# An attention and feed-forward layer on eight cores: first-sequence tokens loaded ahead of the weights, query weights cast on GpSimd, value weights ahead of projection

## The chip, the cores and the metric

The kernel runs on all 8 cores of one Trainium2 chip. Each core takes two of the 16 sequences, by itself; the cores exchange nothing. The metric is the device time of the slowest core in microseconds (us). Each core has TensorE (matmuls), VectorE, ScalarE and GpSimd, and SyncE (SP), which here issues every transfer. The profile calls them PE (PEld for its weight loads), DVE, ACT, POOL and SP.

## The reference

One layer on x of 16 x 2048 x 1024, 32-bit floats. The softmax is over the 1024 x 1024 matrix of channels (one head, summed over the 2048 tokens), and norm follows norm:

```python
x = x + attn(layernorm(x))
x = x + ffn(layernorm(x))

def attn(x, ...):
    h = (x - mu) / sqrt(var + 1e-5) * norm_w + norm_b
    q, k, v = split(h @ qkv_w.T + qkv_b)            # each 2048 x 1024
    w = softmax(einsum('ncq,nck->nqk', q, k / sqrt(2048)), axis=2)
    a = einsum('nqk,nck->ncq', w, v)
    return a @ proj_w.T + proj_b + x

def ffn(x, ...):
    h = fix8(x @ w1 + b1)                           # 1024 -> 4096, multiples of 2^-8
    h = piecewise linear gelu of h (33 points on [-4, 4]), fix8
    return fix8(h @ w2 + b2)                        # 4096 -> 1024
```

## The kernel before, in words

All engines run programs written out by hand, each in its own order, tied by semaphores. The names below are those of the profile.

**Sequence 0, start.** A sequence is 16 tiles of 128 tokens x 1024 channels (512 KB). A tile comes from `xs` into one of six slots of `ring` (32-bit). VectorE takes its statistics (`stats`, L722 and L725), ScalarE the root (L993), VectorE the reciprocal and `nms` = -mean/std (`finish_stats`, L729 and L731), and ScalarE writes the normalised tile to `Z` in 16 bits (L1003), which frees the slot. All slots are used in one order, counted by a position u: position u waits until the user of position u - 6 is done (`wait_slot`). TensorE adds each Z tile to the Gram matrix Z^T Z (L395: 11 matmuls a tile for most of it; a twelfth piece of 16 matmuls follows at the end because it reuses a bank). VectorE evicts it scaled by norm_w into `gm` (L750). GpSimd adds the 16 Z tiles into `acc` (L1200), from which TensorE makes column sums (L411).

**Weights.** The query (`wq`), key (`wk`), projection (`pw`) and value (`wv`) weights come as 8 tiles of 512 KB each through the same six slots and are cast to 16 bits: wq and wk on ScalarE (L1134), pw and wv on GpSimd (L1205). SP issues, in this order: the 16 x tiles with the first 4 wq tiles and nwb (norm_w as 512 KB) between them, the other 4 wq tiles, 8 wk tiles, two rows of biases, 16 stores of Z to `zscr`, `nbb` and `rbb`, 8 pw tiles, 8 wv tiles.

**Stages of sequence 0 on TensorE.** T1 = gm x wq: 16 tiles (L424), the first 8 mixed with transposes of gm (L404) that ScalarE copies back (`mirror`, L1015); VectorE and ScalarE evict T1 in turns. Column sums stand between T1 tiles 11 and 12; VectorE makes the columns `colq`, `colk` of them (L768 to L774). Then matvecs with wq and wk (L432, L439); scores, 8 tiles of 16 + 2 matmuls (L452, L457) in two pairs of banks; for each, VectorE takes the maximum (L797), `mxb` (L800), then `junk` (L814), which multiplies a value-weight tile in its slot by nbb and sums (`bias_v`), and scales the exponentials of ScalarE (L1039) to `wsm` (L806). The M stage (wsm x pw, L470 and L480: the first group of 4 tiles goes through the 8 softmax tiles qt in turn, and needs pw tile qt), then the N stage (M x wv, L501, L513, L520). Then the out stage, 16 tiles (L531) that read the transposed Z, `zt`.

**Sequence 1 beside it.** During M and N of sequence 0, VectorE and ScalarE take statistics and normalise the 16 x tiles of sequence 1, one between each two evictions, and GpSimd sums them. SP stores each Z tile, issues a transposed load (L264, from `zscr` to `zt`, of sequence 0) after every second one, and loads the next x tile. The Gram matrix of sequence 1 and its column sums come just before and between the out tiles of sequence 0 (`gram_slot`). From there to the end of the program (T1, softmax, M, N and out of sequence 1, and the feed-forward of all 32 token tiles) nothing is changed.

A load of a wv tile's slot waits for both its cast (`g_wv`) and its `junk` (`v_bv`).

## Time and profile before

| | before |
|---|---|
| median of 3 runs (lowest, highest) | 1439.39 us (1436.79, 1488.41) |
| profiled execution | 1433.04 us |
| its span, slowest core (3) | 1431.5 us |
| spans of the other cores | 1422.0 to 1429.9 us |
| busy: TensorE, VectorE, ScalarE, GpSimd | 94%, 75%, 57%, 42% |
| mean granted clock of TensorE, core 3 | 0.984 |

The span goes from the first to the last instruction of a core. Times in rows are us from its start. A busy engine is one that executes, and a matmul's end is modelled. "Idle before" names what an engine waited for last. The profile is one execution, of the slowest core.

### The profile page before, as it was taken

What the parts mean: (1) busy time and instruction counts of PE and PEld (TensorE: products, weight loads), DVE (VectorE), ACT (ScalarE), POOL (GpSimd) and SP (SyncE); (2) the same over time, 40 slices, a digit from 0 to 9 for tenths busy, and PEclk for the clock granted to TensorE, in tenths of its full rate; (3) what the DMA queues carried; (4) which work ended last, traced back from release to release, by engine and by line L of the source; (5) the groups of instructions that cost most, each with busy time, mean ns of one, the idle gap of its engine ahead of it and who ended that gap; (6) DMA issues with size and microseconds to landing.
All of it is one profiled execution on the core that took longest, in us unless ns stands there. A gap on an engine that the chain in (4) does not pass through costs nothing.

```text
span 1431.5 us, 22191 instructions; the slowest of 8 cores (1422.0 to 1431.5 us)
## 1 busy us (share of the span) xinstructions
PE 1339.8 (94%) x6232; PEld 603.2 (42%) x6232; DVE 1073.8 (75%) x1664; ACT 813.2 (57%) x1303; POOL 602.7 (42%) x435
## 2 busy tenths in 40 slices
PE   5896998999999977799999999999999999999998
PEld 2342444444444423344444444444444444444443
DVE  5426884553326789998888889889889889888883
ACT  5531552451216756666766766666676765766660
POOL 0814253441646566534443433433443443443430
PEclk9998999999999999999999999999999999999999
DMA  8677696669998851321031021022023013002102
GB/s 271 187 230 238 159 265 205 220 231 203 335 297 288 293 171 45 74 79 33 16 82 52 15 75 60 16 60 74 16 38 95 2 38 95 16 26 64 30 16 96
DMA packets 124540, 171.93 MB, mean 120 GB/s; under 512 B 74620, under 2 KB 74620, under 8 KB 124420
## 3 DMA queue, kind: packets, MB, share of 16 engines
q1 hardware_dynamic: 124420, 170.52, 39.8%
q8 instruction: 52, 0.85, 0.2%
q14 instruction: 68, 0.56, 0.1%
HBM read 103.38 MB, written 50.33 MB: 107 GB/s over the span
## 4 chain that ended last, share of the span: by engine, by line
PE 58%; DVE 19%; issue 13%; DMA 4%; ACT 4%; SPq 1%; DVEq 1%; POOL 0%; ACTq 0%; POOLq 0%
PE pf L643 16%; PE pf L671 9%; PE pf L656 8%; PE pf L531 8%; DVE gb L947 6%; DVE rbits L939 4%; PE pf L452 3%; PE pf L424 3%; DVE rbits L950 3%; PE pf L480 3%; PE pf L395 2%; DVE ub L964 2%; DMA ring<-xs 2%; PE pf L520 1%; DVE bn L722 1%
## 5 line engine op out<-in xcount | busy, mean ns | idle before, releaser
L1246 POOL TENSOR_TENSOR gb<-gb,ga 128x512 f32<-128x512 f32 x256 | 363.7, 1421 | 515.1 <-ACT gb L1102 515.1
L656 PE MATMUL pf<-w,yt 128*128 128x512 bf16 x1024 | 261.2, 384 | 26.5 <-ACT yt L1110 25.0
L1110 ACT ACTIVATE yt<-rbits 128x512 bf16<-128x512 int32 x256 | 160.8, 628 | 213.4 <-DVE rbits L950 213.3
L950 DVE SCALAR_TENSOR_TENSOR rbits<-ga,gb 128x512 int32<-128x512 f32 x256 | 260.2, 1017 | 27.5 <-DVE gb L947 0.9
L643 PE MATMUL pf<-z2cmA,w 128*128 128x512 bf16 x1024 | 244.0, 383 | 16.7 <-ACT kb L1094 16.7
L671 PE MATMUL pf<-w,yt 128*128 128x512 bf16 x1024 | 251.9, 380 | 0.0
L643 PE MATMUL pf<-z2cmB,w 128*128 128x512 bf16 x1024 | 241.9, 379 | 0.0
L1094 ACT ACTIVATE kb<-pf,b1x 128x512 int32<-128x512 f32 x256 | 173.5, 678 | 89.7 <-PE pf L643 88.3
L947 DVE SCALAR_TENSOR_TENSOR gb<-rbits,gb 128x512 f32<-128x512 int32 x256 | 202.4, 791 | 3.3 <-POOL gb L1246 3.2
L939 DVE TENSOR_SCALAR rbits<-kb 128x512 int32<-128x512 int32 x256 | 148.8, 581 | 44.9 <-ACT kb L1094 44.6
L1102 ACT ACTIVATE gb<-kb,c 128x512 f32<-128x512 int32 x256 | 181.0, 707 | 0.0
L656 PEld LDWEIGHTS pf<-w,yt 128*128 128x128 bf16 x1024 | 99.9, 98 | 153.3 <-issue 38.2
L643 PEld LDWEIGHTS pf<-z2cmA,w 128*128 128x128 bf16 x1024 | 100.3, 99 | 143.0 <-issue 27.2
L942 DVE TENSOR_SCALAR kb<-kb 128x512 int32<-128x512 int32 x256 | 136.7, 534 | 27.9 <-DVE rbits L939 1.4
L1101 ACT ACTIVATE ga<-kb 128x512 f32<-128x512 int32 x256 | 157.4, 615 | 0.0
L671 PEld LDWEIGHTS pf<-w,yt 128*128 128x128 bf16 x1024 | 100.5, 98 | 121.8 <-issue 1.7
L643 PEld LDWEIGHTS pf<-z2cmB,w 128*128 128x128 bf16 x1024 | 100.2, 98 | 120.8
L531 PE MATMUL pf<-nn,zt 128*128 128x512 bf16 x512 | 115.1, 385 | 4.7 <-DMA zt<-zscr 3.6
L1205 POOL CAST w<-ring 128x1024 bf16<-128x1024 f32 x64 | 72.3, 1129 | 71.4 <-DMA ring<-w_h 71.3
L395 PE MATMUL pf<-Z 128*128 128x512 bf16 (+3 forms) x384 | 69.5, 340 | 24.9 <-ACT Z L1003 24.9
L1210 POOL TENSOR_TENSOR xo<-xo,rbb 128x1024 f32<-128x1024 f32 x32 | 75.3, 2358 | 15.8 <-ACT xo L1069 15.8
L531 PEld LDWEIGHTS pf<-nn,zt 128*128 128x128 bf16 x512 | 50.5, 99 | 66.7 <-issue 9.4
(93 smaller groups left out, 1108.0 us busy)
## 6 DMA issues: line engine op xcount, KB each, us to landing
ring<-xs SPq DMA_DIRECT2D x64, 512.0 KB, 5.7
ring<-w_h SPq DMA_DIRECT2D x64, 512.0 KB, 8.0
x1scr<-xo SPq DMA_DIRECT2D x32, 512.0 KB, 3.3
xh<-x1scr SPq DMA_DIRECT2D x64, 256.0 KB, 3.3
ys<-xh SPq DMA_DIRECT2D x64, 256.0 KB, 2.2
zscr<-Z SPq DMA_DIRECT2D x32, 256.0 KB, 5.4
z2scr<-z2b SPq DMA_DIRECT2D x32, 256.0 KB, 2.6
ring<-wq_h SPq DMA_DIRECT2D x8, 512.0 KB, 5.1
```

The source lines that it names most:

```text
L531: mm = t.matmul(bank(pair + h), zt[:, d, 128 * m:128 * (m + 1)], nn[:, d, 512 * h:512 * (h + 1)], start=(d == 0), stop=(d == 7))
L643: mm = t.matmul(bank(h_bank(n)), w1[:, 4 * (ft // 4) + j // 2, w1_col(ft, j)], z2cm[c % 2][:, j, :], start=(j == 0), stop=(j == 7))
L656: mm = t.matmul(bank(tt), y_tile(c, ft, tt), w2[:, ft, 0:512], start=(ft == 0), stop=(ft == 31))
L671: mm = t.matmul(bank(HALF1_BANKS[tt % 2]), y_tile(c, 8 * q + r, tt), w2[:, 8 * q + r, 512:1024], start=(r == 0 and q == 0), stop=(r == 7 a ...
L939: v.tensor_scalar(out=rbits[n % 4][:], in0=kb[n % 3][:], scalar1=63, scalar2=None, op0=ALU.bitwise_and).then_inc(S["v_bits"], 1)
L947: v.scalar_tensor_tensor(out=gb[n % 2][:], in0=rbits[n % 4][:], scalar=4.0, in1=gb[n % 2][:], op0=ALU.mult, op1=ALU.mult).then_inc(S["v_mu ...
L950: v.scalar_tensor_tensor(out=rbits[n % 4][:], in0=ga[n % 2][:], scalar=256.0, in1=gb[n % 2][:], op0=ALU.mult, op1=ALU.add).then_inc(S["v_h ...
L1094: a.activation(out=kb[n % 3][:], in_=bank(h_bank(n)), func=AF.Identity, bias=b1x[:, n % 32:n % 32 + 1], scale=256.0).then_inc(S["a_k"], 1)
L1101: a.activation(out=ga[n % 2][:], in_=kb[n % 3][:], func=AF.Gelu, scale=float(2.0 ** -8))
L1102: a.activation(out=gb[n % 2][:], in_=kb[n % 3][:], func=AF.Gelu, bias=c025[:], scale=float(2.0 ** -8)).then_inc(S["a_g"], 1)
L1110: a.activation(out=yt[:, r, q, :, :] if c % 2 == 0 else yt[:, r, :, q, :], in_=rbits[n % 4][:].rearrange("p (a b) -> p a b", a=4), func=AF ...
L1246: g_.tensor_tensor(out=gb[n % 2][:], in0=gb[n % 2][:], in1=ga[n % 2][:], op=ALU.subtract).then_inc(S["g_d"], 1)
```

## The change

The program of SP: all 16 x tiles come first, positions 0 to 15; then the small constants and nwb; then wq, wk, and now wv ahead of pw. nbb and rbb are loaded right behind wk. A wv tile's load is issued after every second store of Z. Two transposed loads stand between pw and the six first x tiles of sequence 1, two behind them, and the other four after the second, fourth, sixth and eighth store of Z of sequence 1. GpSimd casts wq, between additions 7 and 8 of its sum; the sum no longer waits for 13 tiles. ScalarE casts one wk tile after each of its first four T1 evictions and one after each of the other four. VectorE makes the columns after all its T1 evictions, forms nms with tensor_scalar (per-partition scalar sr, constant -1) where it used scalar_tensor_tensor, and finishes tile 0 before it takes the statistics of tile 1.

```diff
@@ sync_program
-                if p in X_AT:
-                    s.wait_ge(S["a_z"], X_AT[p] + 1)
-                elif p in Q_AT:
-                    s.wait_ge(S["a_wq"], Q_AT[p] + 1)
+                if p < U_WQ:
+                    s.wait_ge(S["a_z"], p + 1)
+                elif p < U_WK:
+                    s.wait_ge(S["g_wq"], p - U_WQ + 1)
...
-            for t in range(6):
-                load(x_pos(t), x_tile(t))
+            for t in range(16):
+                load(t, x_tile(t))
             for dst, src in ((ident[:], ident_h), (cols[:], cols_h), (c2[:], c2_h)):
                 s.dma_start(out=dst, in_=src).then_inc(S["d_const"], 16)
-            for t in range(6, 16):
-                load(x_pos(t), x_tile(t))
-                if t in (7, 9, 11, 13):
-                    load(q_pos((t - 7) // 2), wq_h[(t - 7) // 2])
...
-            for j in range(4, 8):
-                load(q_pos(j), wq_h[j])
+            s.dma_start(out=nwb[:], in_=nwb_h).then_inc(S["d_nwb"], 16)
+            for j in range(8):
+                load(U_WQ + j, wq_h[j])
             for j in range(8):
                 load(U_WK + j, wk_h[j])
...
             for t in range(16):
                 s.wait_ge(S["a_z"], t + 1)
                 store_z(t)
...
+                if t % 2:
+                    load(U_WV + t // 2, wv_h[t // 2])
+            for j in range(8):
                 load(U_P + j, p_h[j])
...
-            for j in range(8):
-                load(U_WV + j, wv_h[j])
+            s.wait_ge(S["d_zst"], 256)
+            load_zt(0, range(2))
             for t in range(6):
                 load(U_X1 + t, x_tile(16 + t))
-            s.wait_ge(S["d_zst"], 256)
+            load_zt(0, range(2, 4))
             for t in range(16):
                 s.wait_ge(S["a_z"], 16 + t + 1)
                 store_z(16 + t)
-                if t % 2 == 0:
-                    load_zt(0, [t // 2])
+                if t % 2 and t < 8:
+                    load_zt(0, [4 + t // 2])
@@ vector_program
-                v.scalar_tensor_tensor(out=nms[:, g:g + 1], in0=mv[:, g, 0:1], scalar=-1.0, in1=sr[:, g:g + 1],
-                                       op0=ALU.mult, op1=ALU.mult).then_inc(S["v_nms"], 1)
+                v.tensor_scalar(out=nms[:, g:g + 1], in0=mv[:, g, 0:1], scalar1=sr[:, g:g + 1], scalar2=-1.0,
+                                op0=ALU.mult, op1=ALU.mult).then_inc(S["v_nms"], 1)
...
-            for i in range(1, 12, 2):
+            for i in range(1, 16, 2):
                 t1_evict(0, i)
             columns(0, XB[0][3])
-            for i in (13, 15):
-                t1_evict(0, i)
@@ scalar_program
-                if g in (8, 10, 12, 14):
-                    cast(wq[:, (g - 8) // 2, :], q_pos((g - 8) // 2), "a_wq")
-            for j in range(4, 8):
-                cast(wq[:, j, :], q_pos(j), "a_wq")
...
                 if j % 2:
                     t1_evict(0, 7 - j)
+                    cast(wk[:, (7 - j) // 2, :], U_WK + (7 - j) // 2, "a_wk")
             for i in range(8, 16, 2):
                 t1_evict(0, i)
-                cast(wk[:, i - 8, :], U_WK + i - 8, "a_wk")
-                cast(wk[:, i - 7, :], U_WK + i - 7, "a_wk")
+                cast(wk[:, i // 2, :], U_WK + i // 2, "a_wk")
@@ gpsimd_program
-                if b == 0:
-                    g_.wait_ge(S["a_z"], 13)
...
-            accumulate(0)
+            accumulate(0, range(7))
+            for j in range(8):
+                cast(wq[:, j, :], U_WQ + j, "g_wq")
+            accumulate(0, range(7, 15))
+            for j in range(8):
+                cast(wv[:, j, :], U_WV + j, "g_wv")
             for j in range(8):
                 cast(pw[:, j, :], U_P + j, "g_p")
```

SP's queue where the last x tiles of sequence 0 are issued, before (`ring` is the slots, `xs` x, `wq_h` and `wk_h` the query and key weights; line numbers differ between the two kernels):

```order
L257 DMA ring_69<-wq_h 128x1024 [waits a_wq]
L257 DMA ring_70<-xs 128x1024 [waits a_z]
L257 DMA ring_71<-xs 128x1024 [waits a_z]
L257 DMA ring_72<-wq_h 128x1024 [waits a_wq]
L257 DMA ring_67<-xs 128x1024 [waits a_z]
L257 DMA ring_68<-xs 128x1024 [waits a_z]
L257 DMA ring_69<-wq_h 128x1024 [waits a_wq]
L257 DMA ring_70<-wq_h 128x1024 [waits a_z]
```

And of the change, from the last three x tiles on:

```order
L245 DMA ring_68<-xs 128x1024 [waits a_z]
L245 DMA ring_69<-xs 128x1024 [waits a_z]
L245 DMA ring_70<-xs 128x1024 [waits a_z]
L267 DMA ident<-ident_h 128x128
L267 DMA cols<-cols_h 128x56
L267 DMA c_106<-c_h 2x1
L268 DMA nwb<-nwb_h 128x1024
L245 DMA ring_71<-wq_h 128x1024 [waits a_z]
L245 DMA ring_72<-wq_h 128x1024 [waits a_z]
```

The x tiles moved ahead of all query weights, which now follow in a block of eight whose last two wait for GpSimd's casts (`g_wq`).

SP's queue from the last value-weight tiles to the x tiles of sequence 1, before (`g_wv` counts casts, `v_bv` the `junk` instructions):

```order
L257 DMA ring_70<-wv_h 128x1024 [waits g_p]
L257 DMA ring_71<-wv_h 128x1024 [waits g_wv,v_bv]
L257 DMA ring_72<-wv_h 128x1024 [waits g_wv,v_bv]
L257 DMA ring_67<-xs 128x1024 [waits g_wv,v_bv]
L257 DMA ring_68<-xs 128x1024 [waits g_wv,v_bv]
```

And of the change, from the fourth projection tile (`p_h`) on:

```order
L245 DMA ring_68<-p_h 128x1024 [waits g_wv,v_bv]
L245 DMA ring_69<-p_h 128x1024 [waits g_wv,v_bv]
L245 DMA ring_70<-p_h 128x1024 [waits g_wv,v_bv]
L245 DMA ring_71<-p_h 128x1024 [waits g_p]
L245 DMA ring_72<-p_h 128x1024 [waits g_p]
L252 DMA_TRANSPOSE zt<-zscr 128x2048 [waits d_zst]
L252 DMA_TRANSPOSE zt<-zscr 128x2048
L245 DMA ring_67<-xs 128x1024 [waits g_p]
L245 DMA ring_68<-xs 128x1024 [waits g_p]
```

The waits for `junk` moved from the x tiles of sequence 1 to the projection tiles, and two transposed loads stand before the first of those x tiles.

GpSimd at its start, before (`acc` is the sum, `d_ring` the landing of a slot):

```order
L1200 TENSOR_TENSOR acc<-Z 128x1024 [waits a_z]
L1200 TENSOR_TENSOR acc<-acc,Z 128x1024 [waits a_z,g_acc] x14
L1205 CAST pw<-ring_69 128x1024 [waits d_ring2]
L1205 CAST pw<-ring_70 128x1024 [waits d_ring3]
L1205 CAST pw<-ring_71 128x1024 [waits d_ring4]
```

And of the change:

```order
L1177 TENSOR_TENSOR acc<-Z 128x1024 [waits a_z]
L1177 TENSOR_TENSOR acc<-acc,Z 128x1024 [waits a_z,g_acc] x6
L1182 CAST wq<-ring_71 128x1024 [waits d_ring4]
L1182 CAST wq<-ring_72 128x1024 [waits d_ring5]
L1182 CAST wq<-ring_67 128x1024 [waits d_ring0]
L1182 CAST wq<-ring_68 128x1024 [waits d_ring1]
L1182 CAST wq<-ring_69 128x1024 [waits d_ring2]
L1182 CAST wq<-ring_70 128x1024 [waits d_ring3]
L1182 CAST wq<-ring_71 128x1024 [waits d_ring4]
L1182 CAST wq<-ring_72 128x1024 [waits d_ring5]
L1177 TENSOR_TENSOR acc<-acc,Z 128x1024 [waits a_z,g_acc] x8
L1182 CAST wv<-ring_69 128x1024 [waits d_ring2]
```

Eight casts moved into the sum, and the value casts come right behind it.

## Rows read from the trace of the kernel before

**Rows 1.** Timeline, TensorE: start, length (us), engine, line, operation, out<-in, count [idle before]

```profile
25.70 1.89 PE L395 MATMUL pf<-Z 128*128 128x512 bf16 x11 [0.49 <-ACT Z L1003]
...
46.64 11.49 PE L395 MATMUL pf<-Z 128*128 128x512 bf16 x49 [4.11 <-ACT Z L1003]
...
59.60 0.55 PE L404 MATMUL pf<-ident,gm 128*128 128x128 bf16 x7 [1.47 <-DVE gm L750]
...
81.88 1.84 PE L411 MATMUL pf<-ones,acc 128*128 128x1 f32 x16
...
90.58 3.61 PE L432 MATMUL pf<-wq,colq 128*2 128x512 bf16 x16
...
97.58 3.63 PE L452 MATMUL pf<-wk,t1m 128*128 128x512 bf16 x16
...
122.95 5.70 PE L452 MATMUL pf<-wk,t1m 128*128 128x512 bf16 x16 [12.75 <-ACT eb L1039]
...
145.49 7.08 PE L470 MATMUL pf<-pw,wsm 128*128 128x512 bf16 x32
...
204.20 3.19 PE L395 MATMUL pf<-Z 128*128 128x512 bf16 x14
...
214.96 1.90 PE L411 MATMUL pf<-ones,acc 128*128 128x1 f32 x16
...
220.47 6.42 PE L531 MATMUL pf<-nn,zt 128*128 128x512 bf16 x16 [3.62 <-DMA zt<-zscr]
```

**Rows 2.** Windows: stretch, length, busy time by engine (instructions), clock, DMA, GB/s

```profile
110.00:123.00 13.00, 0.25 (x2) 0.08 (x2) 5.92 (x7) 1.21 (x2) 9.09 (x9) 0.64 1.00 339
...
220.50:227.00 6.50, 6.50 (x19) 2.43 (x20) 0.00 (x0) 0.00 (x0) 0.99 (x1) 0.56 0.76 272
```

**Rows 3.** Timeline, VectorE, x tiles of sequence 0

```profile
17.54 1.29 DVE L722 BATCH_NORM_STATS2 bn<-ring 128x6 f32<-128x512 f32 x2
...
19.47 1.29 DVE L722 BATCH_NORM_STATS2 bn<-ring 128x6 f32<-128x512 f32 x2
```

**Rows 4.** Line 731 alone: VectorE's nms, duration min/median/max in ns, first and last start

```profile
L731 DVE SCALAR_TENSOR_TENSOR nms<-mv,sr x32: 158/160/1700, 9.6 to 209.4; 128x1 f32<-128x1 f32 x32
```

**Rows 5.** Timeline, ScalarE, normalised tiles of either sequence

```profile
21.54 1.24 ACT L1003 ACTIVATE Z<-ring,nms,sr 128x1024 bf16<-128x1024 f32 x1
...
208.74 2.37 ACT L1003 ACTIVATE Z<-ring,nms,sr 128x1024 bf16<-128x1024 f32 x2 [1.33 <-DVE nms L731]
```

**Rows 6.** Timeline, GpSimd: the sum of sequence 0, value-weight casts

```profile
42.97 31.61 POOL L1200 TENSOR_TENSOR acc<-acc,Z 128x1024 f32<-128x1024 f32 x14
...
123.03 3.56 POOL L1205 CAST wv<-ring 128x1024 bf16<-128x1024 f32 x3 [0.58 <-DMA ring<-wv_h]
```

**Rows 7.** Timeline, VectorE: column sums, T1, softmax and N stage

```profile
84.39 0.16 DVE L774 SCALAR_TENSOR_TENSOR colq<-cols,sc 128x8 bf16<-128x8 f32 x1
...
90.75 0.69 DVE L760 CAST t1m<-pf 128x512 bf16<-128x512 f32 x1 [2.76 <-PE pf L424]
...
116.87 2.07 DVE L814 SCALAR_TENSOR_TENSOR junk<-ring,nbb 128x1024 f32<-128x1024 f32 x1 [13.54 <-DMA ring<-wv_h]
...
125.94 0.15 DVE L800 TENSOR_SCALAR mxb<-mx 128x1 f32<-128x1 f32 x1
...
147.09 1.23 DVE L814 SCALAR_TENSOR_TENSOR junk<-ring,nbb 128x1024 f32<-128x1024 f32 x1
...
208.51 0.73 DVE L833 TENSOR_SCALAR nn<-pf,cols 128x512 bf16<-128x512 f32 x1
```

**Rows 8.** Timeline, SP's queue: transposed loads being issued

```profile
172.88 6.83 SPq L264 DMA_TRANSPOSE zt<-zscr  x1
...
316.11 33.08 SPq L264 DMA_TRANSPOSE zt<-zscr  x8
```

**Rows 9.** DMA issues, 0 to 260 us: count, KB each, us to landing

```profile
ring<-xs SPq DMA_DIRECT2D x44, 512.0 KB, 5.3
...
ring<-p_h SPq DMA_DIRECT2D x8, 512.0 KB, 11.2
```

51 lines of the change are left out of this document (20 added, 31 removed).

## The prediction, made before any run of the change

> **What bounds the kernel now.** I read the page first: TensorE is busy 94% of 1431.5 us, so only the places where it waits, or runs at half clock, can give time back. Then I read TensorE's timeline from its start [rows 1], because the change ends where the second sequence is under way. Up to there it loses time in four places. It follows the normalised tiles Z one by one (11 matmuls, 1.89 us, after each) and starts on the fourteenth only at 46.64; the Gram matrix ends at 58.1 and the next stage starts at 59.60. It stands 12.75 us before 122.95, in the score stage. It stands again up to 220.47, for the transposed Z. And after the two long stands the first 16 matmuls take 5.70 and 6.42 us, where 16 at full clock take 3.6: the granted clock was 0.64 of full during the first stand and 0.56 in the 6.5 us behind the second [rows 2], so a good part of those ran at the lower of its two levels (1.2 of 2.4 GHz).
>
> Next, who is waited for. The first loss is the supply of tiles: VectorE could start a tile's statistics every 1.93 us (17.54, 19.47), but four query-weight loads and nwb take places in the load queue between the tiles, and of the 32 nms instructions the longest takes 1.70 us where the median is 0.16: the long ones run while GpSimd sums [rows 3, 4, 6]. The second loss is one VectorE instruction: `junk`, which reads a value-weight tile in softmax tile 0, waits 13.54 us for its load [rows 7]; the value weights stand behind the 16 stores and 8 projection tiles on SP. The third loss is the last of eight transposed loads, plus a Z chain that lags: the N stage's matmuls end at 204.2, its last VectorE eviction starts only at 208.51 and the last Z ends at 211.1 [rows 1, 5, 7]. Behind 220 everything hangs on the out stage of sequence 0 through waits that move with it (w1 and w2 loads are issued after its stores), and nothing there is changed, so a shift at 220 should arrive whole at the end.
>
> **The change, step by step** (E is the end of the scores, N the end of the N stage's matmuls).
>
> 1. *Front.* All 16 tiles come at VectorE's 1.93 us: statistics of tile 15 start at 17.54 + 9 x 1.93 = 34.9. Z of a middle tile ends 5.2 us after its statistics start (17.54 to 21.54 + 1.24) [rows 3, 5]; the last has no following tile to wait through, which saves the 1.3 us of that tile's statistics: 38.8. A 512-column matmul takes 0.216 us in a run (32 in 7.08 less the last one's tail [rows 1]); the eleven of a tile have the columns of eight, 1.73 us, less than 1.93. So TensorE keeps up, then ends tile 15 at 40.5 and the sixteen 512-column matmuls of the last Gram piece at 44.0; with the 1.4 us of handover seen between 58.1 and 59.60 the T1 stage may begin at 45.4, that is 14.2 earlier. The query weights now come behind the tiles and nwb. Their last loads wait for GpSimd's first casts, eight tiles and nwb in a row at 1.55 us a tile (0.524 MB at the 339 GB/s of the fullest stretch [rows 2]): the last lands near 48.4, is cast (1.04 us and a handover) by 49.6, and T1's first tile ends at 49.9, where its seven transposes (0.55) and eight matmuls (1.73) alone would have ended it at 47.7. So 12.0 us are left of 14.2 [rows 1, 6]. Bounds: 14 if the casts keep up, 9 if the x tiles need about 0.3 us more each. The first seven additions of the sum (2.26 each by 31.61/14) and then the casts fit before this, and the other eight take 18.1, to 67.7; the column sums need them at 81.88 - 12.0 = 69.9 [rows 1, 6]. That cover is 2.2 us; beyond it, each late us costs one.
> 2. *Column sums read after all T1 evictions.* The query matvecs (90.58) wait for `columns`, which now stands behind the last eviction (90.75 + 0.69) and lasts 0.7 (83.9 to 84.55): they start at 92.2. Cost 1.6 us [rows 1, 7].
> 3. *Value weights ahead.* Key weights are cast between the mirrors, so value tiles 0 to 5 get slots well before softmax. The stand goes. Score tiles 3 to 7 take 145.49 - 122.95 = 22.54, less 5.70 - 3.63 for the clock, 4.09 each; eight in a row, with the 0.22 that tile 2 waits for the first exponential, take 32.9; they took 145.49 - 97.6 = 47.9. Gain 15.0, the half clock included.
> 4. *Projection weights behind them.* New wait: projection tile 5 takes the slot of value tile 7, so SP issues it after the last `junk`. This is E + 0.1 + 1.22 + 0.15 + 1.23 + handovers = E + 2.8 (145.49 to 148.3) [rows 1, 7]. At the median landing of x tiles, 5.3 us [rows 9], it lands at E + 8.1, tile 7 two places later at 11.2, is cast at 12.4, and the four matmuls of the last group end at E + 13.3. Now they end at E + 6.9. Cost 6.4. Bounds: 4 when the three land together and cast back to back, 12 at the 11.2 us landing that projection tiles have now [rows 9]; I stay near 5.3, since nothing else is in flight then.
> 5. *x tiles of sequence 1.* Behind those three loads SP now issues two transposed loads first (8 take 33.08 us, 4.1 each, the longest single one 6.83 [rows 8]). Tile 16 is then issued at E + 12.2 and lands at 17.5. VectorE and, behind it, ScalarE's next root and eviction wait; M tile 10 needs that eviction at E + 23.7 and has it by about 21.2. Cover 2.5 us, cost 0. Later tiles come two per transposed load, 1 to 3 us late on VectorE, which eight PSUM banks absorb.
> 6. *nms as tensor_scalar.* `mxb`, the same form (tensor_scalar, 128x1), takes 0.15 us at 125.94 while a GpSimd cast runs (three casts, 123.03 to 126.59) [rows 6, 7]; so nms should not wait either. VectorE then keeps up with TensorE: last eviction at N + 0.1 to 0.8, nms by 1.4, last Z at N + 2.9. From the last Z to the end of column sums it is 214.96 + 1.90 - 211.1 = 5.7 [rows 1, 5], so the out stage starts at N + 8.6, with all transposed loads long there; now it starts at 220.47 - 204.2 = 16.3. Gain 7.7. And without the long stand its first tile should run at full clock: 6.42 - 3.6 = 2.8.
> 7. Small collisions (value and projection casts against `junk` and `wsm`; key casts before mirrors on ScalarE): 1.2, an allowance; `junk` beside casts takes 2.07 where it takes 1.23 alone [rows 7], and a score tile leaves VectorE 0.4 us. The first nms made ahead of the second tile's statistics is worth nothing: TensorE gets one tile sooner and then waits for the second.
>
> On the port two sentences of the Trainium skill bear (SBUF — State Buffer, "Who interferes with whom"): a VectorE instruction with two SBUF inputs blocks against a GpSimd instruction that reads SBUF, and the trace agrees (nms up to 1.70 against 0.16 [rows 4]). But the page also lets tensor_scalar enter a 2-port mode that blocks the same way; by that rule nms would still wait, which is the second rival below.
>
> **Sum.** 12.0 + 15.0 + 7.7 + 2.8 = 37.5 gained; 1.6 + 6.4 + 1.2 = 9.2 lost; 28.3 us less. The profiled span goes from 1431.5 to about 1403. Its execution took 1433.0, below the three runs' median of 1439.4, so against the median: 1411.
>
> **Rivals.**
> - *The weights' wait grows* (0.14). Projection tiles land as late as now, or tile 16 beyond its cover: 6 to 10 us more than in steps 4 and 5. About 1420. For it: 5.3 is a median among x tiles, 11.2 the one of these very tiles. Against: those 11.2 were with 16 stores and two more loads in flight.
> - *nms still waits* (0.10). Then nms of a tile waits for the addition that the last Z released: about 2.2 [rows 6] plus Z's own 1.24 [rows 5], a pitch near 3.5 instead of 1.93 for the seven additions that now run during the x loads. That costs 7 x 1.6 = 11, and 3 more in step 6: 1425. Against: `mxb`. For: mxb has no scalar read from SBUF, nms has.
> - *Query weights late* (0.07): loads at 1.9 us each instead of 1.55 and a sum that misses its cover, 5 us: 1416.
> - *Better than the sum* (0.08): projection tiles land together, no collisions: 1405.
> - *Slower* (0.03). Eight transposed loads on SP stand ahead of x tile 13 of sequence 1, and each us more per transposed load delays it by eight. With 5 us each it comes about when needed (3 us of cover). At (28.3 + 3)/8 + 5 = 8.9 us each the whole gain is gone, and from 12.5 each the kernel is slower by 2%: 1468 or more. The longest now is 6.83 [rows 8].
>
> **Numbers.** The forecast has 0.58; its own range is 1405 to 1417. A measurement of this kernel tells about 2%, 28.8 us, from no change, and the forecast lies on that line: half of its chance (0.30) and the better case (0.08) make faster 0.38; the rest of it and the other rivals make the same 0.59; slower 0.03. The range reaches from the lower bounds of steps 1 and 4 to the second rival: 1402 to 1426.
>
> **What would show it.** Step 1: last Z near 39, T1's first tile ending near 49. Step 2: matvecs 1.6 after the last T1 tile. Step 3: no wait of `junk` for a load, scores without a gap. Step 4: a gap of 6 us in the first M group, released by a GpSimd cast. Step 5: VectorE's first statistics of sequence 1 waiting some 5 us for x, with TensorE unhurt. Step 6: all nms near 0.16, the out stage within 9 us of the N stage. Wrong would be: nms above 1 us, a gap in the M stage beyond the first group, or a front that ends later than 53.

## The result, and the profile after

| | before | after |
|---|---|---|
| median of 4 runs each, on one chip | 1439.97 us | 1423.88 us (1422.85 to 1496.78) |
| profiled execution | 1433.04 us | 1423.3 us |
| its span, slowest core | 1431.5 us (core 3) | 1421.8 us (core 4) |
| median span of its eight cores | 1427.1 us | 1416.0 us |

The ratio after to before is 0.9892, with an interval of 0.9874 to 0.991: 1.1% or 15.5 us less (the two medians are 16.1 us apart), faster but by less than 2%. The prediction said 1411 with a range of 1402 to 1426; the forecast's own range, 1405 to 1417, was missed. Span against span, the sum promised 28.3 us and 9.7 came. Since single cores differ by 9 to 10 us, the table below gives the start of each stage as a median over cores. Here and in all that follows, such medians, of stage starts and of spans, leave out cores that ran a whole execution at a granted clock below 0.98, which happened with every kernel, in 10 to 42 of 100 cases; the time of an execution, being that of its slowest core, contains them.

| start, us | T1 stage (first matmul with wq) | query matvecs | M stage | N stage's end | out stage | span |
|---|---|---|---|---|---|---|
| before | 57.4 | 88.0 | 144.1 | 203.0 | 218.2 | 1427.1 |
| after | 48.8 | 83.9 | 123.9 | 190.1 | 207.6 | 1416.0 |

From the out stage to the end both take 1209 us in the median of the cores (1207 to 1212 on single ones), so a shift there does arrive whole at the end, as predicted.

TensorE's timeline of the kernel after, core 4, from its T1 stage to the out stage of sequence 0. The columns are those of [rows 1]: start, duration, line, what it does, count, and in brackets the idle time before it and who ended it.

```profile
49.98 0.55 PE L387 MATMUL pf<-ident,gm 128*128 128x128 bf16 x7 [1.49 <-DVE gm L733]
52.64 0.38 PE L407 MATMUL pf<-wq,gm 128*128 128x512 bf16 x1 [0.81 <-POOL wq L1182]
53.98 0.38 PE L407 MATMUL pf<-wq,gm 128*128 128x512 bf16 x1 [0.97 <-POOL wq L1182]
...
61.12 0.33 PE L387 MATMUL pf<-ident,gm 128*128 128x128 bf16 x3 [0.32 <-ACT gm L998]
...
86.75 5.30 PE L415 MATMUL pf<-wq,colq 128*2 128x512 bf16 x16 [2.44 <-DVE colq L757]
...
95.44 3.63 PE L435 MATMUL pf<-wk,t1m 128*128 128x512 bf16 x16
...
128.46 3.63 PE L453 MATMUL pf<-pw,wsm 128*128 128x512 bf16 x16
133.37 1.02 PE L453 MATMUL pf<-pw,wsm 128*128 128x512 bf16 x4 [1.29 <-POOL pw L1182]
136.66 1.87 PE L453 MATMUL pf<-pw,wsm 128*128 128x512 bf16 x4 [2.27 <-POOL pw L1182]
...
141.73 20.94 PE L463 MATMUL pf<-pw,wsm 128*128 128x512 bf16 x94
...
169.49 1.02 PE L484 MATMUL pf<-mm__51,wv 128*128 128x512 bf16 x4 [0.77 <-ACT mm__51 L1028]
...
194.52 2.75 PE L378 MATMUL pf<-Z 128*128 128x512 bf16 x11
...
201.12 0.59 PE L378 MATMUL pf<-Z 128*128 128x512 bf16 x1 [2.16 <-ACT Z L986]
...
204.79 6.47 PE L378 MATMUL pf<-Z 128*128 128x512 bf16 x33 [0.55 <-ACT Z L986]
...
213.07 3.40 PE L514 MATMUL pf<-nn,zt 128*128 128x512 bf16 x15
```

Against [rows 1]: the stand of 12.75 us in the score stage is gone, and the scores run from 95.44 to 128.46. Two new stands are there for `pw` in the first M group. The N stage ends at 194.5, and then TensorE goes tile by tile behind Z, as it once did at the start; the out stage comes 18.6 us after N's end, where before it came 16.3 after. (Some matmuls can be missing from a trace: x15 where 16 ran.)

The other engines on the same core, in the order of the stages: SP's queue, whose rows say how long an issue held it, then VectorE and ScalarE.

```profile
132.75 8.33 SPq L252 DMA_TRANSPOSE zt<-zscr  x2
141.18 4.17 SPq L245 DMA_DIRECT2D ring<-xs  x6
145.40 13.11 SPq L252 DMA_TRANSPOSE zt<-zscr  x2
158.61 0.53 SPq L248 DMA_DIRECT2D zscr<-Z  x1
159.23 0.38 SPq L245 DMA_DIRECT2D ring<-xs  x1
...
160.13 5.66 SPq L252 DMA_TRANSPOSE zt<-zscr  x1
...
16.25 1.29 DVE L705 BATCH_NORM_STATS2 bn<-ring 128x6 f32<-128x512 f32 x2 [2.52 <-DMA ring<-xs]
...
85.65 0.89 DVE L756 CAST colk<-sc 128x8 bf16<-128x8 f32 x1
...
148.22 1.29 DVE L705 BATCH_NORM_STATS2 bn<-ring 128x6 f32<-128x512 f32 x2 [6.34 <-DMA ring<-xs]
...
165.39 1.29 DVE L705 BATCH_NORM_STATS2 bn<-ring 128x6 f32<-128x512 f32 x2 [2.59 <-DMA ring<-xs]
...
195.08 1.29 DVE L705 BATCH_NORM_STATS2 bn<-ring 128x6 f32<-128x512 f32 x2 [3.53 <-DMA ring<-xs]
...
40.03 2.37 ACT L986 ACTIVATE Z<-ring,nms,sr 128x1024 bf16<-128x1024 f32 x2
...
202.28 2.37 ACT L986 ACTIVATE Z<-ring,nms,sr 128x1024 bf16<-128x1024 f32 x2
```

SP stood in two transposed loads from 145.40 to 158.51. The first store of Z of sequence 1, and the x load that follows it, were behind them. Four more such loads stood between stores (5.66, 5.19, 5.58 and 4.91 us), and VectorE waited six times for an x tile (6.34, 2.59, 2.95, 2.04, 2.14, 3.53 us; three of them shown). So the last Z ends at 204.65, ten us after the N stage.

The nms line of the same core (lowest, median and highest ns), and the engines' busy time in two stretches:

```profile
L714 DVE TENSOR_SCALAR nms<-mv,sr x32: 214/214/216, 7.8 to 203.0; 128x1 f32<-128x1 f32 x32
```

```profile
core 4: us, PE busy (x) PEld busy (x) DVE busy (x) ACT busy (x) POOL busy (x), PEclk, DMA share, GB/s
44.00:54.00 10.00, 6.74 (x37) 2.92 (x35) 6.13 (x12) 0.92 (x1) 7.14 (x8) 1.00 1.02 338
...
195.00:213.00 18.00, 11.98 (x62) 6.45 (x63) 9.80 (x26) 10.48 (x13) 13.38 (x7) 0.72 0.98 331
```

No nms waits any more (up to 1700 ns in [rows 4]). While the query weights land, the DMA engines are full. In the new slow stretch behind N the granted clock is 0.72, and so 33 matmuls of the Gram piece took 6.47 us: the first out tile got its full clock back (15 matmuls in 3.40 us, where before 16 took 6.42 [rows 1]), and the piece ahead of it lost its own: the same 33 matmuls took 3.87 us before, at 211.25.

### The profile page after: what moved, and what is told of

Same layout as the page of the kernel before. It is cut to its first block, busy times and chain, and to the rows that moved or that the text cites. A ratio compares the mean times of both kernels' runs of the same rounds, so it can differ in the third digit from the quotient of the medians.

```text
span 1421.8 us, 22066 instructions; the slowest of 8 cores (1412.6 to 1421.8 us)
## 1 busy us (share of the span) xinstructions
PE 1335.0 (94%) x6108; PEld 602.2 (42%) x6232; DVE 1057.1 (74%) x1664; ACT 806.3 (57%) x1295; POOL 611.0 (43%) x443
## 4 chain that ended last, share of the span: by engine, by line
PE 53%; DVE 20%; issue 14%; ACT 4%; DMA 4%; SPq 3%; DVEq 1%; POOL 0%; another core or an unknown queue 0%; ACTq 0%; POOLq 0%
PE pf L626 16%; PE pf L654 9%; PE pf L639 8%; DVE gb L930 7%; DVE rbits L922 4%; PE pf L514 4%; PE pf L435 3%; PE pf L407 3%; DVE rbits L933 3%; SPq L252 3%; PE pf L378 2%; DVE ub L947 2%; DMA ring<-xs 2%; PE pf L463 1%; PE pf L503 1%
## 5 line engine op out<-in xcount | busy, mean ns | idle before, releaser
L933 DVE SCALAR_TENSOR_TENSOR rbits<-ga,gb 128x512 int32<-128x512 f32 x256 | 263.2, 1028 | 27.5 <-DVE gb L930 0.9
L639 PE MATMUL pf<-w,yt 128*128 128x512 bf16 x1002 | 256.2, 381 | 26.5 <-ACT yt L1093 24.4
L654 PE MATMUL pf<-w,yt 128*128 128x512 bf16 x1005 | 250.2, 381 | 1.0
L626 PEld LDWEIGHTS pf<-z2cmA,w 128*128 128x128 bf16 x1024 | 100.6, 99 | 145.5 <-issue 30.1
L514 PE MATMUL pf<-nn,zt 128*128 128x512 bf16 x500 | 111.6, 379 | 1.8 <-DVE nn L816 1.1
L1187 POOL TENSOR_TENSOR xo<-xo,rbb 128x1024 f32<-128x1024 f32 x32 | 75.3, 2359 | 14.5 <-ACT xo L1052 14.5
```

Of the source, the lines that this page charges most:

```text
L514: mm = t.matmul(bank(pair + h), zt[:, d, 128 * m:128 * (m + 1)], nn[:, d, 512 * h:512 * (h + 1)], start=(d == 0), stop=(d == 7))
L626: mm = t.matmul(bank(h_bank(n)), w1[:, 4 * (ft // 4) + j // 2, w1_col(ft, j)], z2cm[c % 2][:, j, :], start=(j == 0), stop=(j == 7))
L639: mm = t.matmul(bank(tt), y_tile(c, ft, tt), w2[:, ft, 0:512], start=(ft == 0), stop=(ft == 31))
L654: mm = t.matmul(bank(HALF1_BANKS[tt % 2]), y_tile(c, 8 * q + r, tt), w2[:, 8 * q + r, 512:1024], start=(r == 0 and q == 0), stop=(r == 7 a ...
L933: v.scalar_tensor_tensor(out=rbits[n % 4][:], in0=ga[n % 2][:], scalar=256.0, in1=gb[n % 2][:], op0=ALU.mult, op1=ALU.add).then_inc(S["v_h ...
```

## The experiments

Stage starts are medians over the cores of one profile; "to out" is the time from N's end to the out stage, as the difference of the two medians. T1 is its first matmul with wq. The span is the median over all cores of all timed executions; for before it is 1428.6, 1429.0 and 1428.5 on the three chips used, and in the table it stands for the first; where no other is named, differences are against the first profile of after. Times are us.

| kernel | T1 | matvecs | M stage | N's end | to out | span | ratio to before |
|---|---|---|---|---|---|---|---|
| before | 57.4 | 88.0 | 144.1 | 203.0 | 15.2 | 1428.6 | |
| after | 48.8 | 83.9 | 123.9 | 190.1 | 17.5 | 1416.5 | 0.9892 |
| after, again | 47.4 | 83.6 | 123.7 | 189.2 | 17.1 | 1414.3 | 0.9952 (0.9913 to 0.9991) |
| before, nms alone | 56.5 | 87.1 | 142.9 | 201.8 | 15.1 | 1428.7 | 0.9974 (0.9931 to 1.0017) |
| before, wv ahead alone | 57.8 | 88.3 | 128.8 | 195.6 | 14.5 | 1419.2 | 0.9928 (0.9893 to 0.9963) |
| after, nms undone | 59.4 | 94.9 | 134.9 | 203.4 | 17.4 | 1430.0 | 0.9967 (0.9935 to 1.0) |
| after, front undone | 56.5 | 89.9 | 129.9 | 196.1 | 15.3 | 1420.4 | 0.9948 (0.9902 to 0.9994) |
| after, columns undone | 47.4 | 81.0 | 121.0 | 187.5 | 15.4 | 1411.8 | 0.9897 (0.9828 to 0.9966) |
| after, old transposed loads | | | | | | 1415.3 | 0.9913 (0.9855 to 0.9972) |
| after, transposed loads early | 47.4 | 82.6 | 122.7 | 189.6 | 8.6 | 1408.8 | 0.9931 (0.9883 to 0.9978) |
| after, junk early | 47.4 | 83.7 | 124.0 | 182.9 | 8.7 | 1399.0 | |
| the same, timed again | 47.2 | 83.2 | 123.6 | 182.5 | 8.5 | 1398.7 | 0.9914 (0.9866 to 0.9961) |
| all three | 47.3 | 81.3 | 121.4 | 180.2 | 8.6 | 1396.7 | 0.9799 (0.9711 to 0.9887) |

The profile of the kernel with the old transposed loads has no core that counts, so its stages aren't given. The intervals of the ratios are 0.4 to 0.9% to each side, as much as most steps are worth; the spans and the stage starts decide below.

**The value weights ahead, alone, in the kernel before (steps 3 and 4).**

```diff
-        U_WK, U_P, U_WV, U_X1 = 24, 32, 40, 48
+        U_WK, U_WV, U_P, U_X1 = 24, 32, 40, 48
...
-            for j in range(6):
-                load(U_P + j, p_h[j])
-            for j in range(6, 8):
-                load(U_P + j, p_h[j])
             for j in range(8):
                 load(U_WV + j, wv_h[j])
+            for j in range(8):
+                load(U_P + j, p_h[j])
```

> The kernel before with one part of the change alone: value weights ahead of projection weights, transposed loads and front as before. Theory: the stand of 13 us in the scores goes, with the half clock behind it 15 us (scores last 33 us where they last 49 on the median core), and a wait of 7 us comes in the first M group (14 us from the scores' end to its end, 7 before). The rest is unchanged: 8 to 9 us less, about 1431. Rival: the value loads, which still stand behind 16 stores, nbb and rbb, are late all the same: less than 4 us gained. Second rival: the x tiles of sequence 1 come late behind the projection tiles and eat the rest.

The waits for the slots and the order of GpSimd's casts follow the loads. The M stage starts 15.3 us earlier, with the same front: the 15.0 of step 3. Its first group then waits. TensorE's timeline of this kernel, core 5, at the start of the M stage:

```profile
129.12 3.63 PE L468 MATMUL pf<-pw,wsm 128*128 128x512 bf16 x16
133.28 1.02 PE L468 MATMUL pf<-pw,wsm 128*128 128x512 bf16 x4 [0.54 <-POOL pw L1203]
137.99 1.86 PE L468 MATMUL pf<-pw,wsm 128*128 128x512 bf16 x4 [3.69 <-POOL pw L1203]
...
142.59 1.86 PE L468 MATMUL pf<-pw,wsm 128*128 128x512 bf16 x4
```

The group takes 15.1 us here (the next one starts at 144.25), 13.8 in the median, against 6.9 before. So of 15.3 us some 7 are paid back at once, 7.4 are left at N's end, and 8.1 reach the out stage (218.2 to 210.1); the span is 9.8 less. The exchange of these two weights alone brings some three quarters of what the whole change brings (10.6 at the out stage, 12 to 14 in the span).

**nms, undone in the kernel after and done alone in the kernel before (step 6, second rival).**

```diff
-                v.tensor_scalar(out=nms[:, g:g + 1], in0=mv[:, g, 0:1], scalar1=sr[:, g:g + 1], scalar2=-1.0,
-                                op0=ALU.mult, op1=ALU.mult).then_inc(S["v_nms"], 1)
+                v.scalar_tensor_tensor(out=nms[:, g:g + 1], in0=mv[:, g, 0:1], scalar=-1.0, in1=sr[:, g:g + 1],
+                                       op0=ALU.mult, op1=ALU.mult).then_inc(S["v_nms"], 1)
```

> The change with one thing undone: nms is scalar_tensor_tensor again. Theory (second rival of the prediction, as a price): nms now waits for the addition running on GpSimd in the x stage, a pitch near 3.5 us instead of 1.93 for some seven tiles, so the last Z comes 8 to 11 us later and T1 with it, and nms of sequence 1 takes up to 1.5 us; 1432 to 1436. Rival: additions and statistics fall beside each other, nms stays below 0.5 us and the time stays near 1424.

> The kernel before with one part of the change alone: nms as tensor_scalar. Theory: the last three nms of the x stage and those of sequence 1 no longer wait for GpSimd (up to 1.7 us before); Z of sequence 1 then keeps up with the N stage, but the out stage still waits for the last transposed load, which SP issues behind all the others; 2 us less at the front, 0 to 2 at the out stage: 1436 to 1438 where before is 1440. Rival: the lag of the Z chain was what held the out stage: 6 us less.

Undone in after, it costs 10.6 us at the T1 stage, 13.2 at the out stage, 13.5 to 15.7 in the span (against the second profile of after: 12.0 and 14.5 at the two stages). Alone in before it brings 0.9 us at the T1 stage, 1.3 at the out stage, and nothing that the time shows. Its trace says why, as expected: on core 1 the Gram piece behind N now runs in one go (48 matmuls in 7.11 us from 201.13), so Z keeps up, but the out stage still waits for the last transposed load:

```profile
215.56 5.29 PE L531 MATMUL pf<-nn,zt 128*128 128x512 bf16 x16 [5.58 <-DMA zt<-zscr]
```

VectorE's timeline of the kernel with nms undone, core 1, and GpSimd's addition of the same tile:

```profile
24.30 2.07 DVE L714 SCALAR_TENSOR_TENSOR nms<-mv,sr 128x1 f32<-128x1 f32 x1
26.28 1.27 DVE L705 BATCH_NORM_STATS2 bn<-ring 128x6 f32<-128x512 f32 x2
...
28.03 2.07 DVE L714 SCALAR_TENSOR_TENSOR nms<-mv,sr 128x1 f32<-128x1 f32 x1
...
24.22 2.12 POOL L1177 TENSOR_TENSOR acc<-acc,Z 128x1024 f32<-128x1024 f32 x1 [1.61 <-ACT Z L986]
```

nms ends with the addition, at 26.3. The tiles come 3.73 us apart (24.30 to 28.03) instead of 1.93, near the rival's price (3.5). The form of nms and the early sum on GpSimd belong together: the old form was harmless only while the sum began after the thirteenth Z, and the new sum is affordable only with the new form.

**The front undone (step 1).** The load order, the casts of wq on ScalarE, the start of the sum and the order of the first two tiles' statistics are those of before, all else is after's.

```diff
-            for t in range(16):
-                load(t, x_tile(t))
...
-            for j in range(8):
-                load(U_WQ + j, wq_h[j])
+            for t in range(6, 16):
+                load(x_pos(t), x_tile(t))
+                if t in (7, 9, 11, 13):
+                    load(q_pos((t - 7) // 2), wq_h[(t - 7) // 2])
```

> The change with its front undone: x tiles and query weights interleaved as before, query weights cast on ScalarE, GpSimd's sum in one piece after 13 tiles; the rest is the change. T1 starts at 57.4 before and at 48.8 in the change (medians over cores). Theory: T1 starts near 57 again, less 1 to 2 us for the nms form; it then runs 2 to 3 us shorter than in the change, because no query weight is awaited, so that 5 to 6 us are lost: about 1429. Rival: the sum ends later and holds the column sums, another 5 us: 1434.

Against the two profiles of after it costs 7.7 and 9.1 us at the T1 stage, 6.0 and 6.2 at the M stage, 3.8 and 5.1 at the out stage, and 4 to 6 in the span. So part of what the front gains is lost again, 2 to 3 us up to the M stage and 1 to 2 behind it. That the supply of x tiles sets the pace there would explain the second part; this run alone doesn't show it.

**The columns undone (step 2).**

```diff
-            for i in range(1, 16, 2):
+            for i in range(1, 12, 2):
                 t1_evict(0, i)
             columns(0, XB[0][3])
+            for i in (13, 15):
+                t1_evict(0, i)
```

> The change with one thing undone: the columns are made of the column sums between T1 evictions 11 and 13 again, as before. In the change TensorE waits 1.5 us before the query matvecs on seven cores and 2.4 us on core 4, where a GpSimd cast stood beside the small casts, and it ran at half clock there. Theory: the wait goes, 1.5 to 2.5 us less than the change at the scores and at the out stage alike, since the chain through the last `junk` and SP moves with it: about 1422. Rival: the out stage hangs on loads that don't move with it: no difference.

The matvecs start with T1's last matmul. Beside the repeat of after, in which the T1 stage starts at the same 47.4, they start 2.6 us earlier, the M stage 2.7 and the out stage 3.4, and the span is 2.5 less. So in this kernel the order of the columns costs some 2.5 us, not 1.6.

**The transposed loads as before (step 5).**

```diff
-            s.wait_ge(S["d_zst"], 256)
-            load_zt(0, range(2))
             for t in range(6):
                 load(U_X1 + t, x_tile(16 + t))
-            load_zt(0, range(2, 4))
+            s.wait_ge(S["d_zst"], 256)
...
-                if t % 2 and t < 8:
-                    load_zt(0, [4 + t // 2])
+                if t % 2 == 0:
+                    load_zt(0, [t // 2])
```

> The change with one thing undone: the transposed loads are issued after every second store of Z of sequence 1 again, none ahead of the x tiles. Theory (SP's queue holds the x tiles back): the first x tile of sequence 1 lands about 8 us sooner and VectorE no longer waits 6 us before its statistics, but the last transposed load is now late: the out stage starts some 81 us behind the end of the scores, where it is 84 in the change, 1 to 3 us less in all, about 1422. Rival (the x tiles are not held by the transposed loads but by DMA bandwidth): VectorE waits as long as in the change. If instead the old place is simply worse, the out stage starts later and the time is above 1427.

1415.3 against 1414.3 and 1416.5: no difference, where 1 to 3 us were expected. By the time the new order is no better than the old; both keep all eight loads on SP's path between the pw loads and the last x tile. The waits in its trace say more, though its stage starts don't count. On none of the eight cores (granted clock 0.967 to 0.972) did VectorE wait for an x tile of sequence 1, while on the two cores of the repeat of after with such a clock (0.973 and 0.970) it waited 6.5 and 6.3 us for the first and up to 3.7 us for later ones. The out stage waited for the last transposed load instead, 2.4 to 5.6 us on all eight; on core 6:

```profile
220.06 5.18 PE L512 MATMUL pf<-nn,zt 128*128 128x512 bf16 x16 [2.39 <-DMA zt<-zscr]
```

So where the transposed loads stand in the queue decides whether the x tiles are late, as the theory says. The DMA engines carry the same bytes in both kernels, and the rival's wait is absent. What is won at the x tiles is given back at the last transposed load.

**The transposed loads early**, four of them ahead of the last two wv loads and four between pw loads.

```diff
+            s.wait_ge(S["d_zst"], 256)
+            load_zt(0, range(4))
+            for j in (6, 7):
+                load(U_WV + j, wv_h[j])
             for j in range(8):
                 load(U_P + j, p_h[j])
+                if j < 4:
+                    load_zt(0, [4 + j])
```

> The change with the transposed loads of sequence 0 in the time in which SP's queue stands idle for `junk`: four behind the last store of Z, ahead of value tile 6, and one behind each of the first four projection tiles; the x tiles of sequence 1 follow the projection tiles directly. Theory (the transposed loads in SP's queue hold the x tiles): VectorE waits 6 us less for its first x tile, none of the later ones is late, Z ends within 4 us of the N stage, the out stage starts 9 us behind the N stage instead of 17.5: 8 us less than the change. Rival (the x tiles lag because the DMA engines are full): the wait of VectorE for later x tiles stays, less than 3 us gained. Danger to both: projection tiles come later behind transposed loads and lengthen the 14 us of the first M group.

SP's queue and TensorE on core 0:

```profile
88.10 10.95 SPq L252 DMA_TRANSPOSE zt<-zscr  x4
...
142.83 0.34 SPq L248 DMA_DIRECT2D zscr<-Z  x1
```

```profile
121.70 3.63 PE L454 MATMUL pf<-pw,wsm 128*128 128x512 bf16 x16
128.46 1.39 PE L454 MATMUL pf<-pw,wsm 128*128 128x512 bf16 x4 [3.13 <-POOL pw L1183]
...
188.50 7.11 PE L379 MATMUL pf<-Z 128*128 128x512 bf16 x48
...
197.21 3.61 PE L515 MATMUL pf<-nn,zt 128*128 128x512 bf16 x16
```

The first store of sequence 1 is issued at 142.83, 21.1 us behind the end of the scores, where on core 4 of after it was 30.1 behind (158.61). VectorE waited for no x tile of sequence 1 on the four cores that count. The Gram piece runs in one go at full clock, and the out stage comes 8.7 us after N's end: the 8.6 of step 6. The price is a first M group of 15.0 us here and 15.2 in the median, against 12.9 and 13.4 in the two profiles of after. The span is 5.5 to 7.7 less, about what 8.5 to 8.9 less some 2 leaves. This run takes the transposed loads out of the queue and out of the DMA engines' way at once; it doesn't separate the two.

**`junk` early (step 4).** The eight sums over wv move ahead of the softmax, so the last slot that pw waits for comes free over 20 us sooner (the last of the eight starts 21.9 us before the end of the scores on core 5, at 101.97, instead of 1.6 behind it on core 4 of after, at 130.07). SP's order is after's.

```diff
-            for i in range(1, 16, 2):
+            for i in range(1, 12, 2):
                 t1_evict(0, i)
+            bias_v(0)
+            t1_evict(0, 13)
+            bias_v(1)
+            t1_evict(0, 15)
             columns(0, XB[0][3])
             residual_scales(0)
+            bias_v(2)
+            bias_v(3)
             rows(0)
+            bias_v(4)
+            bias_v(5)
             for qt in range(8):
-                softmax_tile(0, qt, lambda: bias_v(qt))
+                softmax_tile(0, qt, lambda: bias_v(6 + qt) if qt < 2 else None)
```

> The change with VectorE's eight `junk` instructions moved: six between the last T1 evictions and the first softmax tile, the last two into softmax tiles 0 and 1. Theory (projection tiles are late only because their slots wait for `junk`): all projection tiles are cast before the scores end, the first M group takes 7 us instead of 14, and the x tiles and transposed loads behind them start some 20 us sooner, so that the out stage starts within 9 us of the N stage: 7 + 8 = 15 us less than the change. Rival: the DMA engines can't bring them sooner or the early `junk` delay evictions or matvecs; less than 5 us gained.

> The changed kernel with the eight junk sums ahead of the softmax, timed in more rounds. Theory (the two transposed loads that stand in SP's queue behind six x loads block it past the end of scores; with the projection weights freed 35 us earlier that block is over before the first Z store of sequence 1 is due): M's first group has no gap (7 us less) and the out stage follows N's end by about 9 us instead of 17.5, so 15 us under the changed kernel run beside it, about 1408 us. Rival (only the group's gap goes, the rest is given back later): 7 us under it, about 1416.

> The changed kernel itself, beside the next two on one chip, so that they can be compared with it and not only with the kernel before. Both theories: 14 to 17 us under the kernel before, about 1424 us.

TensorE's timeline and SP's queue of the second of these runs, core 5:

```profile
83.53 3.61 PE L415 MATMUL pf<-wq,colq 128*2 128x512 bf16 x16 [2.35 <-DVE colq L757]
...
123.85 7.08 PE L453 MATMUL pf<-pw,wsm 128*128 128x512 bf16 x32
130.76 20.88 PE L463 MATMUL pf<-pw,wsm 128*128 128x512 bf16 x96
...
191.27 3.61 PE L514 MATMUL pf<-nn,zt 128*128 128x512 bf16 x16
```

```profile
119.35 13.54 SPq L252 DMA_TRANSPOSE zt<-zscr  x2
136.89 0.35 SPq L248 DMA_DIRECT2D zscr<-Z  x1
```

The first M group is whole (7.08), and the same two transposed loads, as long as in after (13.54 us), are over 4 us before the first store is due. Both halves of the theory come in: against the repeat of after the first M group is 6.5 us shorter in the median and the out stage 8.6 us closer to N's end, and the span 15.6 less on the same chip (1414.3 to 1398.7). The rival (the gap alone, 7 us) is out. The ratios, which go by the slowest core of each execution, don't show this step: 0.9914 here, 0.9892 and 0.9952 for after.

**All three together**: `junk` early, the columns where they were, one transposed load ahead of pw and seven behind the six x loads.

```diff
-                if t % 2:
+                if t % 2 and t < 12:
                     load(U_WV + t // 2, wv_h[t // 2])
+            for j in (6, 7):
+                load(U_WV + j, wv_h[j])
+            s.wait_ge(S["d_zst"], 256)
+            load_zt(0, range(1))
...
-            load_zt(0, range(2, 4))
+            load_zt(0, range(1, 8))
```

> The same with the columns back between the evictions 11 and 13 of T1, and with one transposed load ahead of the projection weights and seven behind the six x loads, none between the x loads after them. Theory: 15 us from the early junk sums as in the run beside it and 2 to 3 us from the columns (the run with the columns alone had its scores 2.9 us earlier), so about 17 to 18 us under the changed kernel, about 1406 us. Rival (seven transposed loads at the 6.4 us each that two took behind x loads hold SP's queue for 45 us, past the first Z store at 151): the x tiles from 22 on come late and it ends 5 to 15 us above the run beside it, 1413 to 1423.

SP's queue and TensorE's timeline of this kernel, core 2, and the Gram matrix of sequence 0 on core 4:

```profile
110.25 25.09 SPq L252 DMA_TRANSPOSE zt<-zscr  x7
135.44 0.53 SPq L248 DMA_DIRECT2D zscr<-Z  x1
```

```profile
188.14 3.40 PE L514 MATMUL pf<-nn,zt 128*128 128x512 bf16 x15
```

```profile
11.18 34.52 PE L378 MATMUL pf<-Z 128*128 128x512 bf16 x189 [11.18 <-ACT Z L996]
```

Seven transposed loads take 25.09 us, 3.6 each, not the rival's 6.4. The store behind them goes out at 135.44, 2.0 us after its Z tile is done (133.48), and VectorE waits for no x tile on this core. The span is 1396.7, which is 2.0 less than with `junk` early alone, 17.6 less than after and 31.8 less than before on the same chip: 2.2%. The ratio of 0.9799 agrees, but its interval (0.9711 to 0.9887) leaves open whether it is more than 2%. Its lowest execution took 1401.6 us, against 1420.06 for after and 1431.85 for before. It beats both kernels. The median execution, with its slowest core, gains less: 1422.81 us, against 1432.96 and 1435.41 on that chip.

## Why the prediction was right, and where its sum was not

The direction, the range and the order of the events were right. The sum was 18.6 us too good (28.3 against 9.7, slowest core against slowest core), and the steps account for it.

That the time still fell into 1402 to 1426 is in part luck. A span 9.7 us shorter, taken from the median of 1440, gives 1430, outside the range; the medians of the executions moved by 16.1. The 1423.9 lies outside the forecast's own 1405 to 1417 and between the times of the first two rivals (1420 and 1425), and neither of these came about as told. The lower end of the range is also not what its text gives: the better bounds of steps 1 and 4 are worth 2.0 and 2.4 us, which makes 1406.6, not 1402.

**Step 1, the front: 4.3 us short on core 4.** The T1 stage starts at 49.98, not 45.4. 2.9 us are x tiles that landed late (2.52 before 16.25, and 0.35 before another): "all 16 tiles come at VectorE's 1.93 us" held in pace, but nothing was allowed for the first loads, and four of the eight cores waited 1.0 to 2.5 us for the fifth tile. Another 1.1 is an error of mine in the last tile: that its Z comes 1.3 us sooner helps nobody, since TensorE has the tile before it still to do. The other 0.6 of the 4.6 I can't place. The last two Z end at 41.2 and 42.4, TensorE then needs 2 x 1.73 + 3.5 us, and so the kernel in which no tile was late (34.52 us without a break, 11.18 to 45.70) ended the Gram matrix 1.7 later than the 44.0 of step 1 and began T1 at 47.2. The query weights were late as said: the first T1 tile took 4.2 us, where 4.5 were predicted. Bounds of 9 to 14 had been given for this step, and 7.7 came; on core 4 the first T1 tile ends at 54.2, where the text had named 53 as the end beyond which it would be wrong. By the medians the start of T1 moved by 8.6 us, not 14.2; 2.6 of the difference is that core 3 of before, from which I had counted, was that much behind the median of its chip (59.60 against 57.0).

**Between step 1 and 2: 1.3 us, forecast only as an allowance.** TensorE waits 0.27, 0.32 and 0.27 us for the mirrors `gm`, which ScalarE makes behind the casts of wk that now stand between them; the other 0.4 are smaller pieces. Step 7 had 1.2 for all collisions.

**Step 2, the columns: 1.6 predicted, 2.44 on core 4, 1.5 to 1.7 on the seven others.** Core 4 had the cast of `colk` at 0.89 us beside a GpSimd cast of wv. What the step did not have: behind this wait the 16 query matvecs of core 4 ran in part at the lower clock (5.30 us, with a granted clock of 0.69 from 86.5 to 92.0, where the seven others took 3.61), 1.7 us more. It doesn't follow each such wait: core 5 of the kernel with `junk` early waited 2.35 us and took 3.61. A wait has its own length and, on some cores, the clock of what follows.

**Step 3, the score stage: right.** 33.0 us (95.44 to 128.46) where 32.9 was predicted.

**Step 4, the projection weights: right.** The first group takes 141.73 - 128.46 = 13.3 us, as predicted to the tenth, by casts of `pw` as predicted. The rival "the weights' wait grows" fell here. That tenth is luck: on the cores of the two profiles of after the group takes 12.0 to 15.5 us (medians 12.9 and 13.4), and the medians of the five other kernels that have it run from 13.3 to 15.2.

**Step 5, the x tiles: this step failed, and it is the largest.** It said "cover 2.5 us, cost 0" for the first tile and "later tiles come two per transposed load, 1 to 3 us late on VectorE, which eight PSUM banks absorb". The first part was about right: tile 16 was issued at E + 12.7 (12.2 predicted), its statistics began at E + 19.8 (17.5), and TensorE lost nothing for it. The mistake is in what I did not hold against SP's queue: two transposed loads right behind six x loads hold it for 13.1 us, not the 8.2 of [rows 8], the four after them for 4.9 to 5.7 each, not 4.1, and the stores of Z and next x loads stand behind them. The first such store went out at 158.61, though its Z tile was done at 153.84. From there VectorE waited 2.0 to 3.5 us before five of the next ten tiles. The first of these, tile 22, whose load was issued at 159.23, is what TensorE lost the 0.77 us for at 169.49, so PSUM did not absorb all of it in the N stage. And the Gram piece of sequence 1 takes Z itself. So the last Z ends at N + 10.1, not N + 2.9: 7.2 us. The prediction had this mechanism, in its last rival ("Slower", 0.03): with 5 us per transposed load, x tile 13 comes about when needed, and each further us delays it by eight. The eight took 42.8 us, 5.35 each, so that rule gives some 3 us, less than half of what came. The runs show it twice, by loads moved into idle time and by the same loads ended sooner: each time the out stage is back at N + 8.7. And with the old order of these loads no x tile is late.

**Step 6, nms: its own claim right, its consequence not.** All 32 take 0.21 us. By the Trainium skill (SBUF — State Buffer, "Who interferes with whom") a tensor_scalar that enters the 2-port mode blocks against GpSimd; the section says that it can enter it, when its operands meet conditions, not that it does, so "nms would still wait" was more than the page gives. On this single-element form no run here shows a wait, and the kernel with the two-input form shows the wait that the same section gives to two SBUF inputs, 2.07 us against 0.16 alone. The second rival is thus settled, and its price of 14 (11 and 3) confirmed by 13.2 and 14.5 against the two profiles of after, of which 10.6 and 12.0 come at the front; the rest is lost in the M and N stages, not behind them as step 6 has it. But the 7.7 us at the out stage became 2.3 us lost (18.6 against 16.3), since the supply of x tiles had taken the place of nms. The 2.8 us of clock were regained at the first out tile and 2.6 of them given away in the Gram piece ahead of it: 6.47 us for 33 matmuls that follow a row of short waits.

**The sum, mended.** 4.3 (front) + 1.3 (mirrors) + 0.8 and 1.7 (columns, clock) + 0.1 (scores) + 1.0 (M and N stages, 0.77 of it tile 22) + 9.9 (7.2 of late Z, 2.6 of clock, 0.1 handovers) less the allowance of 1.2 gives 17.9 of the 18.6. Another 0.5 lies behind the out stage's start, where 2.3 us were gained and 2.8 promised. The first rival (0.14), "the weights' wait grows, or tile 16 beyond its cover", had the right place, with the wrong part of it: not the first x tile but the ones behind.

The time moved by 15.5 us and the span of the profiled executions by 9.7. Over all executions the median core gained 12 to 14 us (1428.6 to 1416.5, where the first is from another set of runs than the second, and 1428.5 to 1414.3 on one chip). The repeat on that chip gave a ratio of 0.9952 (0.9913 to 0.9991) where the first was 0.9892 (0.9874 to 0.991): the two intervals don't meet, so the size of the gain in time is open between 0.5% and 1.1%, while the spans give 0.8% to 1.0%.

## What to carry to other kernels

A step that moves a slow DMA issue is priced at the queue: list what stands behind it there (here stores, and the loads that wait for them), and follow it to the last consumer, not to the first that is covered. When two stands are removed from a chain, look which supplier comes next behind each: nms in its new form was worth 1.3 us in before, where the transposed loads held the out stage anyway, and 13 to 14 in after. The 9 us of the late x tiles and the 6.5 of the projection weights came in only when they were taken out as well: by the spans the change is worth 0.8% to 1.0%, and 2.2% with them and the columns put right. And count a predicted start from the median core, not from the slowest one, which has its own late transfer in it.

## What the runs showed of the hardware

- Transposed loads of 512 KB held SP's queue longer when six x loads stood in front of them: four issued while almost nothing was in flight (DMA engines busy for 0.09 of the 2 us before) took 10.95 us (2.7 each), two behind six x loads 13.11 and 13.54 (6.6 each), seven behind six x loads 25.09 (3.6 each, so the five more than two cost some 2.4 each). That the queue waits for the transfers in front fits these rows; it is inferred. A single plain load or store beside them held the queue for 0.33 to 0.54 us, six x loads in a row for 3.2 to 9.8.
- While the four transposed loads ran (88 to 99 us), the DMA engines were busy for 0.93 of the time and moved 154 GB/s; with plain loads alone, at 44 to 54 us in after, 1.02 and 338.
- A single-element tensor_scalar of VectorE took 0.21 us in all 32 places, beside GpSimd sums or not, and the single-element form with two SBUF inputs 0.16 alone and up to 2.07, until the addition on GpSimd ended. An eight-element cast to 16 bits took 0.89 us beside a GpSimd cast (85.47 to 86.51, core 4) where it took 0.17 on the seven other cores.
- Short waits can lower the clock too: with waits of 1.31, 2.16 and 1.95 us between single matmuls the granted clock of the stretch was 0.72, and 33 matmuls behind them took 6.47 us instead of 3.87; with the long stands it had been 0.64 and 0.56 [rows 2]. Here, where one long wait became several short ones, 2.6 of the 2.8 us of clock that the first out tile got back were lost again.
